# Moving two more experts onto the second accumulator and reshaping the final sum of a routed transformer block

## What is computed

```python
x = x + ga * attention(layernorm(x) * (1 + ca) + sa)
h = layernorm(x) * (1 + cb) + sb
topk_idx, topk_w = route(h)                       # 8 of 64 experts for each token
y = einsum('eci,eih->ech', silu(g) * u, w_down)   # 64 experts x 256 rows x 512
moe = zeros((n, H)).at[rows].add(y_tok)           # scatter-add of the weighted rows
out = x + gb * (moe + shared_mlp(h))
```

## Time and profile before

| what | value |
|---|---|
| median of 3 executions | 1237.82 us (1237.16, 1237.82, 1242.11) |
| profiled execution, own time | 1239.79 us |
| its span, first to last instruction | 1238.0 us |
| TensorE busy in the span | 94% |
| VectorE, ScalarE, GpSimd busy | 79%, 62%, 40% |
| mean granted TensorE clock, share of full speed | 0.979 |

### The profile page before, as it was taken

How to read it: one execution, slowest core, us unless ns; L and a number is a source line. 1 busy time by engine, 2 the same in 40 slices (tenths; PEclk the granted TensorE clock), 3 DMA queues, 4 the chain that set the end, 5 groups by cost and what they waited for, 6 DMA issues and landing times.

```text
span 1238.0 us, 25480 instructions
## 1 busy us (share of the span) xinstructions
PE 1164.9 (94%) x8876; PEld 880.8 (71%) x8876; DVE 973.8 (79%) x1881; ACT 763.3 (62%) x1507; POOL 497.0 (40%) x375
## 2 busy tenths in 40 slices
PE   8988999999998879999898999999999999999996
PEld 4455556555555655555466889999999999999982
DVE  3678786866657888776756888999899999999976
ACT  3456555556665534455564477777777778778741
POOL 1122212121122120200100048888887887878731
PEclk9999999989999898999999999999999999999998
DMA  9480000000000000003004079999999999999988
GB/s 349 155 314 1 2 18 2 10 10 2 14 10 10 10 1 22 1 10 113 1 23 141 13 209 298 296 304 296 293 300 301 299 293 297 302 296 301 297 237 288
DMA packets 77166, 189.93 MB, mean 153 GB/s; under 512 B 11496, under 2 KB 12136, under 8 KB 76832
## 3 DMA queue, kind: packets, MB, share of 16 engines
q1 hardware_dynamic: 46704, 116.27, 27.7%
q0 software_dynamic: 28672, 71.32, 23.3%
q10 hardware_dynamic: 1712, 1.32, 0.3%
HBM read 136.36 MB, written 52.51 MB: 153 GB/s over the span
## 4 chain that ended last, share of the span: by engine, by line
PE 73%; DVE 13%; DVEq 4%; issue 4%; ACT 3%; DMA 2%; POOL 1%; POOLq 0%; SPq 0%; ACTq 0%
PE ps L1316 22%; PE ps L1355 12%; PE ps L1135 8%; PE ps L1302 5%; PE ps L1165 4%; PE ps L1120 4%; PE ps L1053 4%; PE ps L1085 4%; DVE nmax L1597 3%; PE ps L1105 2%; PE ps L1025 1%; PE ps L1152 1%; DMA acc_dram<-y,slots 1%; PE ps L1183 1%; PE ps L1044 1%
## 5 line engine op out<-in xcount | busy, mean ns | idle before, releaser
L722 POOL DMA_INDIRECT acc_dram<-y,slots x128 | 250.2, 1955 | 76.4 <-issue 49.4
L1597 DVE TENSOR_REDUCE nmax<-ps 128x1 f32<-128x512 f32 (+3 forms) x304 | 191.3, 656 | 92.8 <-PE ps L1089 52.3
L831 ACT ACTIVATE probs<-ps 128x512 f32<-128x512 f32 (+1 forms) x320 | 159.2, 554 | 88.1 <-PE ps L1120 87.2
L673 POOL TENSOR_SCALAR_AFFINE_SELECT probs<-probs 128x512 f32<-128x512 f32 x64 | 44.5, 696 | 381.0 <-ACT probs L831 380.9
L707 POOL DMA_INDIRECT xg<-h_dram,slots x128 | 131.5, 1027 | 85.3 <-DVE slots L1788 41.3
L1085 PE MATMUL ps<-kpad,qpT 128*128 128x512 f32 (+3 forms) x384 | 147.8, 453 | 15.2 <-DVE nmax L1597 13.1
L1120 PE MATMUL ps<-qT,kT 98*128 98x512 f32 (+1 forms) x320 | 115.3, 438 | 5.8 <-ACT probs L831 5.5
L1316 PE MATMUL ps<-x_hi,e_gu_hi 128*112 128x256 f32 (+1 forms) x768 | 120.1, 278 | 0.0
L1316 PE MATMUL ps<-x_hi,e_gu_lo 128*112 128x256 f32 (+1 forms) x768 | 119.6, 278 | 0.0
L1799 DVE TENSOR_TENSOR e_gu_lo<-e_gu,e_gu_hi 128x1408 fp32r<-128x1408 f32 x64 | 103.8, 1622 | 8.1 <-ACT e_gu_hi L953 6.7
L1316 PE MATMUL ps<-x_lo,e_gu_hi 128*112 128x256 f32 (+1 forms) x768 | 109.9, 279 | 0.0
(11 more groups left out here) (236 smaller groups left out, 2374.3 us busy)
## 6 DMA issues: line engine op xcount, KB each, us to landing
e_gu<-in_gate_up SPq DMA_DIRECT2D x64, 704.0 KB, 7.3
e_d<-in_w_down SPq DMA_DIRECT2D x64, 224.0 KB, 4.7
acc_dram<-h SPq DMA_DIRECT2D x2, 4608.0 KB, 25.6
e_d<-in_w_down SPq DMA_DIRECT2D x64, 128.0 KB, 5.4
wmod_b<-in_wmod SPq DMA_DIRECT2D x2, 2048.0 KB, 22.0
xg<-h_dram SPq DMA_DIRECT2D x16, 256.0 KB, 6.4
acc_a<-acc_dram SPq DMA_DIRECT2D x8, 512.0 KB, 9.8
acc_b<-acc_dram SPq DMA_DIRECT2D x8, 512.0 KB, 6.8
```

What stands on the lines that cost most here:

```text
L722: pool.indirect_dma_start(out=acc_dram[a], out_offset=bass.IndirectOffsetOnAxis(ap=slots[:, at:at + 1], axis=0), in_=y[e % 2][:, h, :], in ...
L831: act.activation(probs[:, n % PROBS, 2 * pr:2 * pr + 2, off:CW], unit_bank(2 * n + pr)[:, :, off:CW], ACT.Exp).then_inc(s_exp, 1)
L1597: dve.tensor_reduce(nmax[:, 1 if lo else 0, first:first + heads], max_view(n, heads, hi - lo), AX.X, ALU.max, negate=True).then_inc(s_max, 1)
```

## The change

`SERIAL` goes from 2 to 4: experts 60 and 61 go to accumulator 1 as well. Pair 3 (tiles 6 and 7) gets its addition of `acc_b` from TensorE rather than from VectorE: VectorE still adds gated `acc_a` to `xres` (ahead of pair 2 now) and multiplies `acc_b` with the gate, and TensorE adds the two in the PSUM banks of tiles 8 and 9 after ScalarE has copied these. The load of pair 4 of `acc_b` becomes two DMAs of one tile, with VectorE's multiplication by single tiles; pair 3 is loaded ahead of pairs 0 to 2; VectorE's last addition, and the last four stores, are by single tiles, ten stores in all.

```diff
--- before.py
+++ after.py
@@ -28,7 +28,7 @@
 NF = NT // TPF
 RING = 3
 EARLY = 5
-SERIAL = 2
+SERIAL = 4
 ROUND = 6
 ROUNDS = (E - 2) // ROUND
 CW = 256
@@ -299,6 +299,7 @@
             "guh", "gul", "dh", "dl", "shh", "shl", "shg"))
         s_fin = sem("s_fin")
         s_gated_a, s_gated_b, s_sum, s_copied = (sem("s_" + n) for n in ("gated_a", "gated_b", "sum", "copied"))
+        s_begun, s_head_b = sem("s_begun"), sem("s_head_b")
         s_yfree = sem("s_yfree")
 
         s_step = sem("s_step")
@@ -326,8 +327,14 @@
         SUMMED = 8
         SUM_BANK = dict(zip(range(SUMMED, NT), (2, 4, 3, 5, 6, 7, 0, 1)))
         ON_PE = range(SUMMED // TPF, NF)
-        ON_DVE = range(SUMMED // TPF)
-        STORE_ORDER = 4, 5, 0, 6, 7, 1, 2, 3
+        SHARED_SUM = SUMMED // TPF - 1
+        ON_DVE = range(SHARED_SUM)
+        COPIES = (*range(SUMMED, NT), *range(TPF * SHARED_SUM, TPF * SHARED_SUM + TPF))
+        STORE_ORDER = (8, 2), (10, 2), (0, 2), (12, 2), (14, 2), (2, 2), (6, 1), (4, 1), (5, 1), (7, 1)
+
+        def bank_of(t):
+
+            return ps[:, SUM_BANK[t if t in SUM_BANK else t + TPF], :]
 
         def xtile(t):
             return xres[:, t, :]
@@ -629,16 +636,19 @@
                     sp.wait_ge(s_dl, E)
                 sp.dma_start(first_part(c), av[0][:, TPF * c:TPF * c + TPF, :]).then_inc(s_acc_a[c], 16)
             sp.wait_ge(s_added[1], 16 * HALVES * adds_before(E, 1))
-            for c in (*ON_PE, *ON_DVE):
+            head = ON_PE[0]
+            sp.dma_start(acc_b[:, head, 0, :], av[1][:, TPF * head, :]).then_inc(s_head_b, 16)
+            sp.dma_start(acc_b[:, head, 1, :], av[1][:, TPF * head + 1, :]).then_inc(s_acc_b[head], 16)
+            for c in (*ON_PE[1:], SHARED_SUM, *ON_DVE):
                 sp.dma_start(acc_b[:, c, :, :], av[1][:, TPF * c:TPF * c + TPF, :]).then_inc(s_acc_b[c], 16)
             ov = out.rearrange("(t p) n -> p t n", p=P)
-            for c in STORE_ORDER:
-                if c in ON_PE:
-                    sp.wait_ge(s_copied, TPF * (c + 1) - SUMMED)
+            for t, n in STORE_ORDER:
+                if t + n - 1 in COPIES:
+                    sp.wait_ge(s_copied, COPIES.index(t + n - 1) + 1)
                 else:
-                    sp.wait_ge(s_fin, c + 1)
-                sp.dma_start(ov[:, TPF * c:TPF * c + TPF, :], xres[:, TPF * c:TPF * c + TPF, :]).then_inc(s_out, 16)
-            sp.wait_ge(s_out, 16 * NF)
+                    sp.wait_ge(s_fin, t + n)
+                sp.dma_start(ov[:, t:t + n, :], xres[:, t:t + n, :]).then_inc(s_out, 16)
+            sp.wait_ge(s_out, 16 * len(STORE_ORDER))
 
 
         @block.gpsimd
@@ -1012,9 +1022,9 @@
                 weighted(E - 2 + p, p)
             gates(LAST + 1, 1)
             hidden_hi(LAST + 1, 1)
-            for t in range(SUMMED, NT):
-                act.wait_ge(s_sum, t - SUMMED + 1)
-                act.activation(xtile(t), ps[:, SUM_BANK[t], :], ACT.Copy).then_inc(s_copied, 1)
+            for k, t in enumerate(COPIES):
+                act.wait_ge(s_sum, k + 1)
+                act.activation(xtile(t), bank_of(t), ACT.Copy).then_inc(s_copied, 1)
 
 
         @block.tensor
@@ -1453,7 +1463,7 @@
             down_last(FRONT + 1, 1)
 
             def add_to(t, what, start, stop):
-                return pe.matmul(ps[:, SUM_BANK[t], :], ident, what, start=start, stop=stop)
+                return pe.matmul(bank_of(t), ident, what, start=start, stop=stop)
 
             pe.wait_ge(s_hidden, LAST + 4)
             for t in range(SUMMED, NT):
@@ -1462,10 +1472,16 @@
                 pe.wait_ge(s_gated_a, c - ON_PE[0] + 1)
                 for k in range(TPF):
                     add_to(TPF * c + k, first_part(c)[:, k, :], False, False)
-            for c in ON_PE:
-                pe.wait_ge(s_gated_b, c - ON_PE[0] + 1)
-                for k in range(TPF):
-                    add_to(TPF * c + k, second_part(c)[:, k, :], False, True).then_inc(s_sum, 1)
+            for t in range(SUMMED, NT):
+                pe.wait_ge(s_gated_b, t - SUMMED + 1)
+                add_to(t, second_part(t // TPF)[:, t % TPF, :], False, True).then_inc(s_sum, 1)
+            pe.wait_ge(s_begun, 1)
+            for k in range(TPF):
+                t = TPF * SHARED_SUM + k
+                pe.wait_ge(s_copied, k + 1)
+                add_to(t, xtile(t), True, False)
+                pe.wait_ge(s_gated_b, NT - SUMMED + 1)
+                add_to(t, second_part(SHARED_SUM)[:, k, :], False, True).then_inc(s_sum, 1)
 
 
         @block.vector
@@ -2016,14 +2032,27 @@
             add_gated(1, s_acc_a, first_part(1))
             hidden(LAST + 1, 1)
             hidden_lo(LAST + 1, 1)
+            head = ON_PE[0]
             for c in ON_PE:
                 gated(c, s_acc_a, first_part(c)).then_inc(s_gated_a, 1)
+            add_gated(SHARED_SUM, s_acc_a, first_part(SHARED_SUM)).then_inc(s_begun, 1)
             add_gated(2, s_acc_a, first_part(2))
-            add_gated(3, s_acc_a, first_part(3))
-            for c in ON_PE:
-                gated(c, s_acc_b, second_part(c)).then_inc(s_gated_b, 1)
-            for c in ON_DVE:
-                add_gated(c, s_acc_b, second_part(c)).then_inc(s_fin, 1)
+            dve.wait_ge(s_head_b, 16)
+            dve.tensor_tensor(second_part(head)[:, 0, :], second_part(head)[:, 0, :], gb[:, head // (NF // B), :], ALU.mult)\
+               .then_inc(s_gated_b, 1)
+            dve.wait_ge(s_acc_b[head], 16)
+            dve.tensor_tensor(second_part(head)[:, 1, :], second_part(head)[:, 1, :], gb[:, head // (NF // B), :], ALU.mult)\
+               .then_inc(s_gated_b, 1)
+            for c in ON_PE[1:]:
+                gated(c, s_acc_b, second_part(c)).then_inc(s_gated_b, TPF)
+            gated(SHARED_SUM, s_acc_b, second_part(SHARED_SUM)).then_inc(s_gated_b, 1)
+            for c in ON_DVE[:-1]:
+                add_gated(c, s_acc_b, second_part(c)).then_inc(s_fin, TPF)
+            gated(ON_DVE[-1], s_acc_b, second_part(ON_DVE[-1]))
+            dve.drain()
+            for k in range(TPF):
+                t = TPF * ON_DVE[-1] + k
+                dve.tensor_tensor(xtile(t), xtile(t), second_part(ON_DVE[-1])[:, k, :], ALU.add).then_inc(s_fin, 1)
 
 
 def shape_constants(np):
```

## The result

Over 21 executions each, the median is 1242.07 us with the change and 1238.98 us without: a ratio of 1.0026, 95% interval 1.0018 to 1.0034, so **3.2 us slower** (2.2 to 4.2). That is clear of zero, but within the 0.5% that the prediction called no change, and close to its +2.7. The median of 1242.07 lies in its range of 1238 to 1243, 1.6 us above its 1240.5; 1.2 of these are the kernel before, whose median of three executions was 1237.82 and of 21 is 1238.98. The profiled execution after took 1240.67 us, its span is 1238.9. What it shows inside is not what the prediction added up.

What follows compares the result with a forecast made beforehand. It took the end as a DMA-bound block of 23.9 us behind the last landing of a serial chain of adds. +2.9 for the chain and -0.2 for the stores gave 1237.8 + 2.7 = 1240.5 us, own range 1238 to 1243.

Steps and rivals of the forecast that it cites:

- SERIAL = 4: Chain of adds to accumulator 1: four serial steps instead of two make the last add land 2.9 us later.
- shared sum, single stores: End of the kernel: TensorE's added work is hidden behind DMA, and a smaller last store gains 0.2 us.
- Expert 60 is loaded throughout: 10.3.: Chain of adds: expert 60's step runs beside acc_a loads throughout and takes 10.3 us, the mean of two loaded steps.
- For 61 ... I take 8.9 ... 62 and 63 meet nothing: 8.0 each.: Chain of adds: 61 meets the loads' end, 8.9 us; 62 and 63 run without other traffic, 8.0 us each.
- The bound of 7.1: Chain of adds: an unloaded step would take 7.1 us if expert 62's shorter issue spacing of 1.86 us were the rule.
- L63: Landing of expert 63's adds, after which the acc_b loads begin: 1214.1 before, forecast at 1217.0, 2.9 us later.
- a ninth is under the data: SP's queue, acc_b loads: issuing one more load, about 0.5 us, is hidden under the data movement.
- y of 63: VectorE's queue: expert 63's y waits for 61's landing, at most 3.0 us later, near 1200.7 instead of 1197.7.
- Rival 1: End of the kernel: unloaded steps take 7.1 us and TensorE becomes the bound, 0.9 us less, 1236.9; chance 0.20.
- Rival 2: TensorE's clock falls in the wait before down_last of group 7, 9.0 us more, 1246.8; chance 0.10.
- Rival 3: Chain of adds: three steps run beside dragging acc_a loads, last landing +6.6 us, kernel 1244.2; chance 0.10.
- Rivals 4 and 5: Chain: serial waits cost nothing, 1236.9, chance 0.01. End: TensorE's sum and DMA block shrink over 6.2 us, 0.03.

Runs made afterwards that it cites:

- e1: The kernel before with SERIAL = 4 alone, its end left as it was: +0.9 us (-0.6 to +2.3) against the kernel before.
- e5: The changed kernel with the first load of acc_b as one pair again: +0.9 us (-0.2 to +2.1) against the kernel before.
- e8: The changed kernel with SERIAL = 2, first acc_b load one pair and last four stores as two pairs: +1.0 us (-0.2 to +2.4) against the kernel before.
- e2: The changed kernel with SERIAL back at 2, so only the reshaped end: +1.6 us (0.0 to 3.1) against the kernel before.
- e7: The changed kernel with its last four single-tile stores as two pairs: +2.7 us (1.5 to 4.0) against the kernel before.
- e6: The kernel before with only the first load of acc_b cut into two single tiles: +1.7 us (0.4 to 3.0).
- e9: The kernel before with only the last load of acc_b cut into two single tiles: -0.5 us (-2.0 to +0.9).
- e10: The kernel before with all eight loads of acc_b as sixteen single tiles: -0.5 us (-2.1 to +1.1).
- e12: The kernel before, SERIAL = 2, with acc_a loads paced to at most two queued: -1.5 us (-3.2 to +0.2).
- e11: The kernel before with SERIAL = 4 and each acc_a load issued only when the one before has landed: +4.3 us (2.5 to 6.2).
- e3: The kernel before with SERIAL = 0, so no serial step, and the old end: +9.0 us (6.9 to 11.2).
- e4: The changed kernel with SERIAL = 0, so no serial step, and the reshaped end: +9.0 us (6.6 to 11.5) against the kernel before.

## Why the prediction was right, and where it was not

The time and the sign were right, and so was "no change" within 0.5%. The sum was not: three of its terms were off, one far too high and two too low. That the total came out was luck. From the table, with each edit read in every pair of kernels that differs in it:

| term | predicted | ratios | blocks or chains |
|---|---|---|---|
| SERIAL = 4 | +2.9 | +0.9 (e1), 0.0 (e5 against e8), +1.6 (after against e2); mean +0.8 | chain 44.5 (after, e1, e5, e7) against 43.7 (before, e2, e6, e8): +0.8 |
| two single first loads | 0 | +1.7 (e6), +2.2 (after against e5), +0.6 (e2 against e8); mean +1.5 | block 25.7 (after, e2, e6, e7) against 24.3 (before, e1, e5, e8): +1.4 |
| shared sum, single stores | -0.2 | +1.0 (e8), +0.1 (e5 against e1), -0.1 (e2 against e6); mean +0.3 | block 24.6 (e5, e8) against 24.1 (before, e1): +0.5 |

Each single figure is uncertain by over 1 us; the means add up to 2.6 us of the 3.2 measured. The first and the last term are not clear of zero; that the two single loads cost something is. The split is therefore an estimate. (e8 has paired stores, a difference that e7 does not resolve. e9 and e10 are left out of the means; they too have SERIAL = 2, with chains of 43.6 and 42.6.)

- **Four steps in series, where there were two.** Right: 60 to 63 each start 0.27 us after the landing ahead of them. Of experts 60 and 61 only 60 changes its accumulator, 61 is odd and was on number 1 already; so the change moves one expert, not the two that the section on the change names. The count of four waits stands, as 60 now waits for 59, and 61 for 60.
- **"Expert 60 is loaded throughout: 10.3."** In e1 10.5 from start to start less the hand-over of 0.27, so 10.2: right there; 9.3 in the trace after.
- **"For 61 ... I take 8.9 ... 62 and 63 meet nothing: 8.0 each."** This is the step that failed. They took 7.6, 7.7 and 7.1 us after. The loads did run on as forecast, to about 1194, so the adds of 61 met them for their first 3 us, and cost no more for it:

```profile
1190.00:1192.00 2.00, 2.00 (x20) 2.00 (x19) 1.50 (x2) 0.69 (x1) 1.32 (x1) 1.00 1.05 409
1192.00:1194.00 2.00, 2.00 (x20) 2.00 (x19) 1.60 (x2) 0.65 (x2) 1.70 (x2) 1.00 1.09 371
1194.00:1196.00 2.00, 2.00 (x11) 1.65 (x10) 1.61 (x3) 1.81 (x4) 1.10 (x1) 1.00 0.88 138
```

The 8.0 of expert 63 in the earlier trace rows was read rightly, and most kernels with SERIAL = 2 repeat it: 7.4 to 8.1 in seven traces. With SERIAL = 4 it does not carry over, 63 takes 7.1 to 7.7. One difference seen is the first add's issue, 2.51 us in the earlier trace rows and 1.55 to 1.80 with SERIAL = 4; why is open, and e12 has 1.55 with a step of 7.8. The bound of 7.1, from the spacing of 62's adds, was nearer. From the start of 60 to L63 I had 36.0 us, the traces have 32.5 (after) and 33.8 (e1). That 59 landed 0.5 us later than taken (8.15 instead of 7.7) gives a little back.
- **"a ninth is under the data".** The edit costed at nothing was about half of the loss. The bytes are the same and SP's issue is hidden, but the DMA engines moved less at the start of the loads, 0.5 us' worth in the trace after and 0.7 in e6. The sum had the rate of the block as a constant. What makes up the rest of the longer block is open.
- **Shared sum hidden, VectorE's gain worth nothing.** Right: e8 shows VectorE done 1 us earlier with full DMA engines and no gain. That it costs 0.3 to 0.5 us is not resolved.
- **y of 63.** Forecast near 1200.7, it came at 1198.4, since 61 landed at 1198.3. The wait exists (1.25 us on VectorE) and stays inside the slack.
- **Rival 1** had the better step length, but TensorE does not become the bound: its last copy ends at 1231.7, VectorE's last addition at 1233.2. **Rival 2** fell: the wait before `down_last` of group 7 was 1.45 us, and the granted clock was 1.00 in every window to 1234. **Rival 3** fell: three steps do not meet the loads, and of the two that do only the first is long. (In e11, where the loads are stretched, the second step is the long one, 11.1.) **Rivals 4 and 5** did not come about; the four waits on a landing are in the trace.

## What to carry to other kernels

A total that comes out right proves no term: run each edit alone, and read the two lengths on either side of a clear event (here the landing of the last add) rather than the span. A duration read from one instance carries the state around it: the 8.0 of expert 63 did not hold once the experts ahead of it were in series too, and a neighbour's spacing, used here only as a bound, was the better price. An edit that leaves the bytes alone can still change the rate at which a bandwidth-bound stretch starts, and before a wait is removed (e3), list what is queued behind the next wait on each engine.

## What the runs showed of the hardware that had not been expected

- The rate of a stream of loads from HBM depended on how it began. Over the first 12 us the five kernels with two 256 KB loads ahead of seven of 512 KB moved 295 to 314 GB/s (after, e2, e4, e6, e7), those with eight of 512 KB or with the small ones last 331 to 334 (before, e1, e3, e5, e8, e9, e12), and sixteen of 256 KB 327 (e10). With the small ones last or everywhere there was no loss of time that could be measured. So the mixed start is shown to cost, and its cause is open.
- An accumulating indirect DMA pair of 2 x 256 KB took 8.9 to 11.3 us from first issue to landing beside the queued `acc_a` loads (before, after, e1, e10) and 7.1 to 8.1 us alone. What in the loads delays the adds stays open: the pair of expert 61 began beside 371 to 409 GB/s in the trace after and took 7.6. Pacing the loads is not shown to help (e12), and one at a time went with a step of 11.1 us (e11).
